# A graph network's last convolution: bias in PSUM, norm in the one-hot, one relu for four steps, one-hots shared by POOL and ScalarE; POOL makes the last pieces of the first finish

## What is computed

```
x = emb_table[batch]                      # all rows equal x[0]
for W, b in ((W1, b1), (W2, b2)):
    h = x * norm_src[:, None]
    agg = segment_sum(h[src], dst) * norm_dst[:, None]
    x = relu(agg @ W + b)
```

## Time and profile before

| | us |
|---|---|
| median of 3 runs (9626.31 to 9630.82) | 9628.49 |
| the profiled execution | 9620.59 |
| its span, first to last instruction | 9618.8 |
| first finish (first L1335 to last L1347) | 2483.6 to 2692.4 |
| convolution (first to last start of L2202) | 8533.6 to 9494.1 |
| last finish (first L2289 to last L2295) | 9498.8 to 9616.9 |

### The profile page before, as it was taken

The page is one execution under the profiler, slowest core; times in us unless marked ns, Lnnn a source line. Parts: engine busy times, 40 slices in busy tenths (PEclk is TensorE's granted clock), DMA queues, the critical chain, the costliest instruction groups (busy, mean ns, idle before and its releaser), DMA issues.

```text
span 9618.8 us, 177781 instructions
## 1 busy us (share of the span) xinstructions
PE 7522.0 (78%) x39083; PEld 5959.4 (62%) x39083; DVE 7553.0 (79%) x24798; ACT 6550.1 (68%) x18648; POOL 6596.2 (69%) x7636
## 2 busy tenths in 40 slices
PE   4444444554699999999899999788888888848888
PEld 3333444444467777888688777566666666636665
DVE  7766666666889998666577777788888888899999
ACT  6777777777877775111288866688888888746665
POOL 0377777777257777777577777666666666559994
PEclk6555555555899999999999999655555555567786
DMA  3222222222477777888777742322222222110000
GB/s 54 50 53 54 53 52 53 52 53 53 146 270 256 257 254 278 318 327 321 271 260 256 250 134 66 79 50 50 49 50 50 49 50 49 43 26 1 1 1 28
DMA packets 499509, 1146.59 MB, mean 119 GB/s; under 512 B 149534, under 2 KB 352994, under 8 KB 478894
## 3 DMA queue, kind: packets, MB, share of 16 engines
q0 software_dynamic: 212688, 491.92, 19.1%
q10 hardware_dynamic: 21888, 497.76, 13.4%
q1 hardware_dynamic: 263902, 145.55, 5.6%
HBM read 888.41 MB, written 252.74 MB: 119 GB/s over the span
## 4 chain that ended last, share of the span: by engine, by line
PE 34%; DVE 19%; POOL 17%; ACT 13%; issue 11%; DVEq 2%; DMA 2%; SPq 1%; ACTq 0%; POOLq 0%
PE banks L1419 16%; POOL onehot L2202 9%; POOL step_data L1761 7%; PE banks L2059 4%; ACT banks L1181 3%; PE banks L2069 2%; DVE keys L1105 2%; PE banks L1405 2%; PE banks L1045 2%; ACT onehot L1034 2%; DVE keys L1114 2%; ACT onehot L1032 2%; PE banks L2063 2%; DVE step_small L2033 2%; DVE keys L2039 1%
## 5 line engine op out<-in xcount | busy, mean ns | idle before, releaser
L1020 POOL DMA_INDIRECT gather_ring<-mean_rows,step_data x1660 | 1597.9, 963 | 744.4 <-issue 321.8
L1045 PE MATMUL banks<-gather_ring,onehot 128*128 128x130 f32 x3320 | 950.8, 450 | 1128.0 <-DVE arena L1078 953.2
L1045 PEld LDWEIGHTS banks<-gather_ring,onehot 128*128 128x128 f32 x3320 | 792.6, 301 | 1279.8 <-issue 1030.8
L1419 PE MATMUL banks<-arena 128*128 128x384 bf16 x8232 | 1553.6, 328 | 30.6 <-DMA arena<-split_out 26.6
L1419 PE MATMUL banks<-arena,keys 128*128 128x384 bf16 x8134 | 1528.9, 327 | 3.3 <-DMA arena<-split_im 3.3
L1419 PEld LDWEIGHTS banks<-arena 128*128 128x128 bf16 x8232 | 1134.6, 138 | 266.8 <-issue 35.0
L1419 PEld LDWEIGHTS banks<-arena,keys 128*128 128x128 bf16 x8134 | 1120.0, 138 | 232.6 <-issue 5.1
L1761 POOL DMA_INDIRECT step_data<-next_rows,window_idx x992 | 946.4, 954 | 354.3 <-issue 300.2
L1452 POOL DMA_INDIRECT step_data<-hidden,window_idx x924 | 895.8, 969 | 321.6 <-issue 267.6
L1983 POOL DMA_INDIRECT gather_ring<-attention_rows,step_data x834 | 786.7, 943 | 415.3 <-PE banks L2059 262.2
L1983 POOL DMA_INDIRECT keys<-attention_rows,step_data x826 | 779.2, 943 | 384.1 <-PE banks L2059 283.7
(11 more groups left out here) (316 smaller groups left out, 19353.4 us busy)
## 6 DMA issues: line engine op xcount, KB each, us to landing
keys<-count_rows ACTq DMA_DIRECT2D x48, 3136.0 KB
arena<-count_rows ACTq DMA_DIRECT2D x48, 3136.0 KB
count_rows<-arena ACTq DMA_DIRECT2D x25, 3136.0 KB
count_rows<-keys ACTq DMA_DIRECT2D x25, 3136.0 KB
gather_ring<-mean_rows,step_data POOLq DMA_INDIRECT x1660
step_data<-next_rows,window_idx POOLq DMA_INDIRECT x992
step_data<-hidden,window_idx POOLq DMA_INDIRECT x924
gather_ring<-attention_rows,step_data POOLq DMA_INDIRECT x834
```

Of the source, the lines that this page charges most:

```text
L1020: e.indirect_dma_start(ring_at(rings.slot(name, i), SUM_COLS, SUMS - 1), None, rows, bass.IndirectOffsetOnAxis(src_idx[:, i:i + 1], 0), bo ...
L1045: e.matmul(pass_bank[i % N_SUM_BANKS][:, 0:SUMS], onehot[:, i % STEP_SLOTS, :], ring_at(rings.slot(name, i), SUM_COLS, SUMS), start=True, ...
L1419: m = e.matmul(pass_bank[n % 2][:, 0:SPLIT_COLS], counts[t % 2][:, :, h], split[:, h, :], start=(h == 0), stop=(h == NODE_TILES - 1))
```

## The change

- **Convolution, bias.** VectorE copies `b1` once into PSUM bank 7 (`bias_row`), and lines read it there. PSUM banks for products go from 8 to 7, and an add comes 12 steps after its line instead of 4.
- **Norm in the one-hot.** The source's norm multiplies the one-hot instead of the message. POOL compares and multiplies in one instruction.
- **One-hots shared.** Of five steps POOL makes three one-hots and ScalarE two (`BY_SCALAR`), each as `relu(norm - norm * |iota - place|)` in two activations; the second takes scale and bias from tiles and waits for the first. Each has 8 slots.
- **Relu.** ScalarE applies relu to four steps at once, 512 columns, in 4 slots of four steps; before the relu of group g it makes its one-hots up to those of group g+2.
- **First finish.** The second rest and the third piece (L1259, L1288) move to POOL, which does both for each tile in turn.
- **Last finish.** TensorE's turn waits for the add of tile t-8 (`tile_end`), VectorE's L2267 for its own norm's result, and the norm's result for the store's landing.

```diff
         for now in ends0():
-            if (t := due(now, 17, NODE_TILES, 2)) is not None:
-                e.wait_ge(piece_made[2], t + 1)
-                e.tensor_tensor(halves(rest_many[:, t % 4, :]), halves(rest_many[:, t % 4, :]),
-                                pieces_many[:, t % 8, :, 1, :], ALU.subtract).then_inc(piece_made[3])
...
-            if (t := due(now, 18, NODE_TILES, 2)) is not None:
-                e.wait_ge(piece_made[3], t + 1)
-                e.activation(pieces_many[:, t % 8, :, 2, :], halves(rest_many[:, t % 4, :]),
-                             ACT.Copy).then_inc(piece_made[4])
...
+    def finish0_gpsimd(e):
+        for t in range(NODE_TILES):
+            e.wait_ge(piece_made[2], t + 1)
+            e.tensor_tensor(halves(rest_many[:, t % 4, :]), halves(rest_many[:, t % 4, :]),
+                            pieces_many[:, t % 8, :, 1, :], ALU.subtract).then_inc(piece_made[3])
+            e.wait_ge(piece_made[3], t + 1)
+            e.tensor_copy(pieces_many[:, t % 8, :, 2, :], halves(rest_many[:, t % 4, :])).then_inc(piece_made[4])
...
-    CONV_SLOTS, CONV_LAG = 8, 4
+    CONV_BANKS, CONV_LAG = 7, 12
+    RELU_STEPS, RELU_SLOTS = 4, 4
+    CONV_TURN, CONV_HOTS = 5, 8
+    BY_SCALAR = (2, 4)
+    bias_row = tile_bank[3][:, 0:D]
...
     def conv_gpsimd(e):
-        for j in range(STEPS):
-            if j >= CONV_SLOTS:
-                e.wait_ge(step_summed, STEPS + j - CONV_SLOTS + 1)
-            e.tensor_scalar(onehot[:, j % CONV_SLOTS, :], iota_row[:, :], dst_local[:, j:j + 1], None,
-                            ALU.is_equal).then_inc(hot_made)
+        e.wait_ge(a_coefs, 2 * DRAWS)
+        for p, j in enumerate(pool_steps):
+            if p >= CONV_HOTS:
+                e.wait_ge(step_summed, STEPS + pool_steps[p - CONV_HOTS] + 1)
+            e.tensor_scalar(onehot[:, p % CONV_HOTS, :], iota_row[:, :], dst_local[:, j:j + 1], edge_norm[:, j:j + 1],
+                            ALU.is_equal, ALU.mult).then_inc(hot_made)
 
     def conv_vector(e, regs):
+        e.wait_ge(a_coefs, 2 * DRAWS)
+        for i, k in enumerate(BY_SCALAR):
+            e.tensor_scalar(norm_minus.rearrange("p (t k) -> p t k", k=len(BY_SCALAR))[:, :, i],
+                            edge_norm[:, 0:STEPS].rearrange("p (t k) -> p t k", k=CONV_TURN)[:, :, k], -1.0, None,
+                            ALU.mult).then_inc(conv_ready)
+        e.tensor_copy(bias_row, l3b1[:, :]).then_inc(conv_ready)
+        e.wait_ge(conv_ready, 3)
...
-                if j >= CONV_SLOTS:
-                    e.wait_ge(conv_messages, j - CONV_SLOTS + 1)
-                e.scalar_tensor_tensor(lines[:, j % CONV_SLOTS, :], first_row[:, :], edge_coef[:, j:j + 1], l3b1[:, :],
-                                       ALU.mult, ALU.add).then_inc(conv_lines)
+                if k == 0 and g >= RELU_SLOTS:
+                    e.wait_ge(conv_messages, g - RELU_SLOTS + 1)
+                e.scalar_tensor_tensor(lines[:, g % RELU_SLOTS, k * D:(k + 1) * D], first_row[:, :],
+                                       edge_coef[:, now:now + 1], bias_row, ALU.mult, ALU.add).then_inc(conv_lines)
...
+    def conv_hot_scalar(e, k):
+        if k >= CONV_HOTS:
+            e.wait_ge(step_summed, STEPS + scalar_steps[k - CONV_HOTS] + 1)
+        e.activation(hot, iota_row[:, :], ACT.Abs, bias=dst_local[:, j:j + 1], scale=-1.0).then_inc(conv_far)
+        e.wait_ge(conv_far, k + 1)
+        e.activation(hot, hot, ACT.Relu, bias=edge_norm[:, j:j + 1], scale=norm_minus[:, k:k + 1]).then_inc(conv_near)
 
     def conv_scalar(e):
+        for g in range(RELUS):
+            ahead = min((g + 3) * RELU_STEPS * len(BY_SCALAR) // CONV_TURN, len(scalar_steps))
+            for k in range(made, ahead):
+                conv_hot_scalar(e, k)
+            made = ahead
+            e.wait_ge(conv_lines, (g + 1) * RELU_STEPS)
+            if g >= RELU_SLOTS:
+                e.wait_ge(step_summed, STEPS + (g - RELU_SLOTS + 1) * RELU_STEPS)
+            e.activation(messages[:, g % RELU_SLOTS, :], lines[:, g % RELU_SLOTS, :], ACT.Relu).then_inc(conv_messages)
...
     def finish4_tensor(e):
                 if t >= 8:
-                    e.wait_ge(row_stored[t % 8], stored(STORES4, t - 8, 8))
+                    e.wait_ge(tile_end, lap(2, t - 8))
```

More of the change, by code:

```diff
@@ L491, in program @@
     conv_lines = sem("convolution_line_made")
-    conv_messages = sem("convolution_message_made")
+    conv_messages = sem("convolution_messages_made")
+    conv_ready = sem("convolution_constants_made")
+    conv_far = sem("convolution_distances_made")
+    conv_near = sem("convolution_onehots_made")
     score_steps = sem("score_split_steps")
@@ L2205, in conv_vector @@
-    def conv_vector(e, regs):
+    CONV_BANKS, CONV_LAG = 7, 12
+    RELU_STEPS, RELU_SLOTS = 4, 4
+    CONV_TURN, CONV_HOTS = 5, 8
+    BY_SCALAR = (2, 4)
+    RELUS = STEPS // RELU_STEPS
+    lines = gather_ring[:, :].rearrange("p (b c) -> p b c", b=RELU_SLOTS)
+    messages = keys[0][:, LANE - GATHER_WORDS:].rearrange("p (b c) -> p b c", b=RELU_SLOTS)
+    bias_row = tile_bank[3][:, 0:D]
+    scalar_hot = turned_few[:, :, :].rearrange("p s c -> p (s c)").rearrange("p (s e) -> p s e", s=CONV_HOTS)
@@ new lines, in program @@
+    scalar_steps = [j for j in range(STEPS) if j % CONV_TURN in BY_SCALAR]
+    pool_steps = [j for j in range(STEPS) if j % CONV_TURN not in BY_SCALAR]
+    scalar_place = {j: k for k, j in enumerate(scalar_steps)}
+    pool_place = {j: p for p, j in enumerate(pool_steps)}
+    norm_minus = window_idx[:, STEPS:STEPS + len(scalar_steps)].bitcast(F32)
+    def conv_gpsimd(e):
+        e.wait_ge(a_coefs, 2 * DRAWS)
[4 more added lines that the diff above has]
+                            ALU.is_equal, ALU.mult).then_inc(hot_made)
@@ L2208, in conv_vector @@
         for now in range(STEPS + CONV_LAG):
             if now < STEPS:
[L2210 to L2214 removed]
+                g, k = divmod(now, RELU_STEPS)
+                if k == 0 and g >= RELU_SLOTS:
+                    e.wait_ge(conv_messages, g - RELU_SLOTS + 1)
@@ L2222, in conv_vector @@
                 e.wait_ge(step_summed, STEPS + j + 1)
-                e.tensor_tensor(part, part, bank_all[j % CONV_SLOTS][:, 0:D], ALU.add).then_inc(step_added)
-    def conv_scalar(e):
[L2226 to L2231, removed]
+                e.tensor_tensor(part, part, bank_all[j % CONV_BANKS][:, 0:D], ALU.add).then_inc(step_added)
+    def conv_hot_scalar(e, k):
+        j = scalar_steps[k]
+        hot = scalar_hot[:, k % CONV_HOTS, :]
+        if k >= CONV_HOTS:
[3 more added lines that the diff above has]
+        e.activation(hot, hot, ACT.Relu, bias=edge_norm[:, j:j + 1], scale=norm_minus[:, k:k + 1]).then_inc(conv_near)
+    def conv_scalar(e):
+        e.wait_ge(conv_ready, 3)
+        made = 0
+        for g in range(RELUS):
[7 more added lines that the diff above has]
+            e.activation(messages[:, g % RELU_SLOTS, :], lines[:, g % RELU_SLOTS, :], ACT.Relu).then_inc(conv_messages)
     def conv_tensor(e):
@@ L2235, in conv_tensor @@
         for j in range(STEPS):
[L2236 to L2240, removed]
+            g, i = divmod(j, RELU_STEPS)
+            if j >= CONV_BANKS:
+                e.wait_ge(step_added, STEPS + j - CONV_BANKS + 1)
+            if j in scalar_place:
+                e.wait_ge(conv_near, scalar_place[j] + 1)
+                hot = scalar_hot[:, scalar_place[j] % CONV_HOTS, :]
+            else:
+                e.wait_ge(hot_made, 2 * STEPS + pool_place[j] + 1)
+                hot = onehot[:, pool_place[j] % CONV_HOTS, :]
+            e.wait_ge(conv_messages, g + 1)
+            e.matmul(bank_all[j % CONV_BANKS][:, 0:D], hot, messages[:, g % RELU_SLOTS, i * D:(i + 1) * D],
                      start=True, stop=True).then_inc(step_summed)
```

8 lines of the change are left out of this document (4 added, 4 removed).

## The result

The changed kernel takes 9525.9 us (median of four runs, 9522.3 to 9534.5) where the kernel before, run beside it, takes 9627.4 us (9616.3 to 9630.8): a ratio of 0.9901, 95% interval 0.9889 to 0.9912. The profiled execution took 9522.7 us, its span is 9520.8 for 9618.8. I had forecast 9499 us and a range of 9482 to 9568; the gain is 98 us between the two profiles where I had 129.

What follows compares the result with a forecast made beforehand. POOL's one-hots were taken to bound the convolution, then VectorE at 0.499 us a step. Saving 127 us there and 2 in the first finish from 9620.6 gives 9491.6, plus 7.9 to the median: 9499 us, range 9482 to 9568.

Steps and rivals of the forecast that it cites:

- The stretch: Convolution, VectorE's line: the 0.12 us a step that appears beside POOL's one-hots goes with the bias in PSUM, leaving 0.46.
- The register load: Convolution, VectorE: loading eight tile offsets every eighth step adds 0.31 us, making 0.499 us a step.
- Stalls: Convolution: stalls of the engine that POOL covers cost 2 us.
- POOL's one-hot: Convolution: compare and multiply in one instruction takes 0.7 us, 0.42 a step with three of five one-hots.
- Rivals 2 and 3: Convolution: POOL's two-operation one-hot sets the step above 0.83 us (9567, 7%), or slows it above 0.965 us (9818, 4%).
- ScalarE: Convolution: a dependent pair of activations takes 0.80 us, with the relu 0.45 us a step, under VectorE's 0.499.
- rival 1: Convolution: ScalarE becomes the bound; at 0.53 us a step it saves 81 us instead of 133, giving 9551 us; 17%.
- Start of the stage: Convolution: the lag of 12, ScalarE's first one-hots and the small copies start the adds some 4 us later.
- The first finish: First finish: SP's store issues keep the pace at 1.96 us a tile, POOL's part takes 1.5; saving 2 us.
- rival 5: First finish: POOL slows it by 10 to 33 us on top of the forecast, 9510 to 9535 us; 9%.
- The last finish: Last finish: VectorE alone still sets 1.16 us a tile, so the saving is 0.
- the likeliest case: Whole kernel: the forecast itself, 9499 us, with its own range 9484 to 9518 us and a 60% chance.

Runs made afterwards that it cites:

- experiment 8: The kernel before with only the bias put in a PSUM bank, seven banks left for messages: convolution 955.6 us for 961.3, ratio 0.9993 to the kernel before.
- experiment 4: The changed kernel with the line reading its bias from SBUF again: convolution 885.5 us, ratio 0.9941 to the changed kernel's side of the bank, interval 0.9917 to 0.9966.
- Experiment 3: The changed kernel with all convolution adds at one constant address, so no register loads and incomplete output: convolution 765.7 us, ratio 0.9837 to the kernel before.
- experiment 1: The changed kernel with each register load bringing four tile offsets instead of eight: convolution 855.0 us, ratio 0.9917 to the kernel before.
- (6): The changed kernel with each register load bringing two tile offsets instead of eight: convolution 1090.9 us, ratio 1.0106 to the kernel before.
- (12): The changed kernel with two tile offsets packed per word, one four-word load serving eight steps: convolution 832.3 us, ratio 0.9891 to the kernel before.
- (5): The changed kernel with each register load bringing one tile offset instead of eight: convolution 1097.4 us, ratio 1.011 to the kernel before.

## Why the prediction came out as it did

**What bounds the kernel before: right.** POOL made one-hots every 0.579 us, and experiment 8 shows that this was its own pace, not contention. VectorE's rhythm under it was read from the last steps as 0.46 us; it is 0.455 throughout.

**The stretch: right.** It went from all lines, and went again with the bank alone (experiment 8). That PSUM was needed for it is not shown: in experiment 4, without the bank, POOL paid instead, 22 us.

**The register load: mis-sized, and most of the miss.** The term 0.31 in (8*0.46+0.31)/8 is the one that failed. I took the extra 0.31 us from the earlier trace rows: add 0.57 us behind its line for 0.27. In the earlier trace rows that line is one of 0.46 us, stretched, and the load had started ahead of the add before. I removed the stretch in one term of the sum and used a row with the stretch in another. It is 0.903-0.455 = 0.45 us: 207*(0.448-0.31) = 29 us more than forecast. Experiment 3 took 97 us away, which is 207*0.45 = 93 and a part of the next term.

**Stalls, 2 us forecast.** 1452*0.455+207*0.903 is 847.6 us of the 863.1; 15.5 are left. 50 gaps of 0.60 to 0.66 us make 8.5 of them, as from 8557.25 to 8557.88 here, 9 load steps of about 1.26 us make 3, and 8 gaps of about 0.77 us make 2.5:

```profile
8557.25 0.29 DVE L2244 TENSOR_TENSOR arena<-arena,banks 128x128 f32 x1
...
8557.88 0.29 DVE L2244 TENSOR_TENSOR arena<-arena,banks 128x128 f32 x1
```

They come every 25 steps (the next gap of this size begins at 8570.2, 13.0 us later), whatever the other engines do. The step has five instructions on this queue, so 25 steps and their three loads are 128. The count holds in other runs: with 5.25 a step (experiment 1) they come every 24 to 25 steps, with 5.5 (6) every 23 to 24, with 5.6 (12) every 22 to 23, with 6 (5) every 21 to 22. That it is the supply of instructions is argued from this count, not tried. In the kernel before, POOL's pace covers most of them.

The rhythm gave 8 us back (0.455 for 0.46, 1660 times), so the convolution is 828+29+15-8 = 864 us, measured 863.

**POOL's one-hot: off by a tenth, without effect.** 0.78 us for the 0.7 I took; the turning point was 0.83. Rivals 2 and 3 fall, but the margin was less than half of what I thought: POOL is 90% busy, not 80, and experiment 3 ran into it at 0.46 us a step.

**ScalarE: right.** From one activation to its dependent one it is 0.42 us, to the next pair 0.40: 0.82 for 0.80; it is 89% busy for 90, and it waits for lines, so rival 1 falls. Experiment 3 drives it at 0.46 us a step.

**PE: right in effect.** It waits for banks, and its granted clock in the stretch rose from 0.79 to 0.97.

**Start of the stage: right.** 4 us forecast, 4.1 found from POOL's first one-hot to the first add. That the first add comes only 0.9 us later than before is luck: the stages that the change leaves alone ran 4.2 us shorter in this execution.

**The first finish:** 2 us forecast, none found (1.0 longer), and rival 5 falls: POOL's two instructions take 0.78 and 0.44 us. What I held for VectorE's room is mostly used up beside them: from 2520 to 2680 us it is busy 147.0 us for 152.8 before, though one instruction of 0.33 us a tile is gone. Groups of the first finish, after (busy, mean ns, idle before):

```profile
L1314 POOL TENSOR_TENSOR keys<-keys 128x256 f32<-128x256 f32 x98 | 76.4, 780 | 85.1 <-ACT keys L1287 85.1
L1264 DVE TENSOR_TENSOR keys<-keys 128x256 f32<-128x256 f32 x98 | 46.7, 476 | 0.8 <-ACT keys L1293 0.8
L1278 DVE SCALAR_TENSOR_TENSOR keys<-arena,keys 128x128 f32<-128x128 f32 x98 | 46.0, 470 | 1.6 <-ACT keys L1305 1.6
L1317 POOL CAST keys<-keys 128x256 bf16<-128x256 f32 x98 | 43.4, 443 | 6.3
```

The same two of VectorE took 418 and 284 ns in the kernel before. The 470 is a mean of two kinds: the median is 287 ns, the longest 759.

**The last finish: right.** Tiles are 1.16 us apart, as in the earlier trace rows:

```profile
9508.82 0.33 DVE L2311 SCALAR_TENSOR_TENSOR keys<-banks,norm_dst,l3b 128x128 f32<-128x128 f32 x1
...
9509.98 0.33 DVE L2311 SCALAR_TENSOR_TENSOR keys<-banks,norm_dst,l3b 128x128 f32<-128x128 f32 x1
```

So the bound and the sign were right, the time 27 us too low, outside the likeliest case's own 9484 to 9518 and inside the range. (By its own two terms, 5 us and 0.495 a step, the low end was 9487.) Between the profiles 31 us are missing: 33 in the stretch of adds (863 us for 830) and 3 in the first finish, less 4 by the luck above and 1 at the end. Of my own signs two fell: the adds span 863 us and POOL is busy 90%. The third stands on its edge: I had written that the forecast fails as a whole if adds come more than 0.52 us apart, and they come 0.5203 apart.

## What to carry to other kernels

When a step stops being the bound, price what it covered from a place where the cover is already absent, and take every term of the sum from the same conditions: a row with stretched lines in it cannot price a kernel without them. Where each instruction of an engine waits for the one before it, measure that loop first; independent work that fits between two of them can be nearly free and should be spread out, not gathered. A sequencer's load of registers on such a loop is paid by what it reads: of the sizes tried four words at a time were best, and more in a word was better still.

## What the runs showed of the hardware

- A load of registers from SBUF on VectorE's sequencer: 303 ns for one word, 525 for two, 346 for four, 596 for eight, 2101 for thirty-two.
- POOL's compare over 128x128 takes 0.577 us from one to the next, compare and multiply 0.773.
- Where the line of VectorE and the one-hot of POOL both read SBUF, one is stretched by about 0.12 us: the line in the kernel before (0.46 for 0.34, in 73% of the steps), POOL in experiment 4 (0.908 for 0.791).
- On VectorE, 128x128 f32: a line starts 0.20 us after an add, the next instruction 0.26 us after a line; two adds with registers for addresses, the second waiting for the first, are 0.42 us apart.
- VectorE, with a wait from each add to the next, has a stall of about 0.16 us in an ordinary step and 0.35 in a load step once in 128 instructions of its queue, in five runs with 5.1 to 6 instructions a step.
